# Scattering expert results to a row per pick, norms by chunks, and counts in bf16 at the tail of a four-layer transformer kernel

## The reference

```
x = _layernorm(x + _L0_attn_ref(x, ...))     # causal attention, 16 heads
x = _layernorm(x + _L0_ffn_ref(x, ...))      # 6 layers of window attention and feed-forward
x = _layernorm(x + _L1_attn_ref(x, ...))     # circular memory
x = _layernorm(x + _L1_ffn_ref(x, ...))      # routed experts
```

```
bound = _circ_conv(x, bind_key)
hologram = jnp.einsum('ts,bsd->btd', decay_matrix, bound)    # d ** (t - s) for s <= t
retrieved = _circ_corr(hologram, unbind_key)
```

```
probs = jax.nn.softmax(xf @ router_w.T, axis=-1)
topw, topi = jax.lax.top_k(probs, K)
topw = topw / (topw.sum(-1, keepdims=True) + 1e-06)
...                                          # sort by expert and weight, rank < capacity is kept
eo = jnp.einsum('ecf,efd->ecd', jax.nn.silu(g) * u, wd)
out = jnp.zeros_like(xf).at[st].add(gathered * (sw * keep)[:, None])
```

## Time and profile before

| | |
|---|---|
| three runs | median 2456.55 us (2451.24 to 2464.27) |
| profiled execution | 2461.72 us, span 2459.9 us |
| busy in the span | PE 2049.9 us (83%), DVE 1858.0 (76%), ACT 1636.6 (67%), POOL 1226.2 (50%) |
| first 2193 us | not touched by the change |
| 2193.6 to 2257.4 us | residual, norm b, memory, norm c |
| 2257.4 to 2323.5 us | routing |
| 2323.5 to 2403.2 us | the eight experts |
| 2403.2 to 2459.9 us | gathering the results, last norm, store |

### The profile page before, as it was taken

How to read it: one execution, slowest core, us unless ns; L and a number is a source line. 1 busy time by engine, 2 the same in 40 slices (tenths; PEclk the granted TensorE clock), 3 DMA queues, 4 the chain that set the end, 5 groups by cost and what they waited for, 6 DMA issues and landing times. The chain is left out here.

```text
span 2459.9 us, 55624 instructions
## 1 busy us (share of the span) xinstructions
PE 2049.9 (83%) x20371; PEld 1369.4 (56%) x20371; DVE 1858.0 (76%) x3667; ACT 1636.6 (67%) x3009; POOL 1226.2 (50%) x1091
## 2 busy tenths in 40 slices
PE   4389889638999999999999999999999999843390
PEld 2133333214677776777766767766767766632260
DVE  4555663249999999999999999999999999524523
ACT  2035655427888888888888888888888888712020
POOL 0100000047766777776777776677776677300115
PEclk8569997769999999999999999999999999966595
DMA  2403110031110112110211011111211011003102
GB/s 80 89 5 40 26 17 3 3 128 34 36 36 28 36 36 76 32 36 28 81 36 36 28 60 51 33 36 36 72 36 36 28 36 36 27 17 92 50 29 55
DMA packets 70913, 103.25 MB, mean 42 GB/s; under 512 B 21686, under 2 KB 45884, under 8 KB 70108
## 3 DMA queue, kind: packets, MB, share of 16 engines
q1 hardware_dynamic: 68980, 96.29, 14.4%
q0 software_dynamic: 1664, 3.41, 0.6%
HBM read 41.66 MB, written 8.06 MB: 20 GB/s over the span
## 5 line engine op out<-in xcount | busy, mean ns | idle before, releaser
L755 PE MATMUL pA<-layer_weights,x_feature_major 128*128 128x512 f32 x768 | 399.9, 603 | 32.3 <-DMA window_mask<-in_mask_dram 16.2
L1328 POOL TENSOR_TENSOR qk<-rot_cos,rot_sin 128x512 f32<-128x512 f32 x256 | 323.4, 1274 | 155.7 <-DVE rot_sin L1129 155.7
L399 ACT ACTIVATE probs_by_key<-pT 128x512 f32<-128x512 f32 (+3 forms) x384 | 177.6, 490 | 225.8 <-PE pT L352 192.3
L1127 DVE TENSOR_TENSOR rot_cos<-pA,layer_tab 128x512 f32<-128x512 f32 x384 | 262.9, 685 | 77.6 <-ACT sq L968 71.4
L1338 POOL TENSOR_TENSOR qk<-qk,rnorm 128x512 f32<-128x512 f32 x256 | 263.4, 1045 | 88.7 <-DVE rnorm L1162 88.7
L417 DVE TENSOR_REDUCE minus_max<-pS 128x1 f32<-128x1024 f32 (+7 forms) x256 | 184.6, 754 | 128.0 <-PE pS L326 127.8
L968 ACT ACTIVATE sq<-pA 128x512 f32<-128x512 f32 x384 | 228.7, 596 | 67.7 <-PE pA L755 58.1
L1139 DVE TENSOR_REDUCE sumsq<-sq 128x8 f32<-128x512 f32 x384 | 253.6, 671 | 15.3 <-ACT sq L968 15.2
L1129 DVE TENSOR_TENSOR rot_sin<-pA,layer_tab 128x512 f32<-128x512 f32 x384 | 260.9, 680 | 0.0
L1028 ACT ACTIVATE probsT<-pD 64x512 f32<-64x512 f32 x384 | 226.6, 590 | 44.5 <-PE pD L796 41.0
L1345 POOL TENSOR_TENSOR probs<-probs,row_inverse 128x1024 f32<-128x1024 f32 x96 | 182.6, 1903 | 101.7 <-DVE row_inverse L1198 101.7
(11 more groups left out here) (281 smaller groups left out, 4447.4 us busy)
## 6 DMA issues: line engine op xcount, KB each, us to landing
v_shifted<-v SPq DMA_DIRECT2D x96, 384.0 KB, 3.5
v_shifted<-v SPq DMA_DIRECT2D x95, 128.0 KB, 3.4
layer_weights<-in_Wqkv_dram SPq DMA_DIRECT2D x24, 384.0 KB
q_stack<-stacked SPq DMA_DIRECT2D x72, 64.0 KB
k_stack<-stacked SPq DMA_DIRECT2D x72, 64.0 KB
stacked<-part SPq DMA_DIRECT2D x24, 128.0 KB, 1.9
layer_weights<-in_Wo_dram SPq DMA_DIRECT2D x6, 512.0 KB
w_gate<-in_wg_dram SPq DMA_DIRECT2D x8, 256.0 KB, 6.4
```

What stands on the lines that cost most here:

```text
L755: pe.matmul(A[c % 2][:, :], cols(X0f, s), slot(s, QKV_AT + 512 * c, 512), start=True, stop=True).then_inc(q_ready[c], 1)
L1127: dve.tensor_tensor(t1[c % 2][:, :].rearrange("p (h g d) -> p h g d", g=2, d=32), a, tabl[s % 2][:, j].unsqueeze(1).broadcast_to([P, 8, 2, ...
L1328: pool.tensor_tensor(qk(s, c), t1[c % 2][:, :], t2[c % 2][:, :], ALU.add).then_inc(added[c], 1)
```

## The change

It has three parts.

- `add_aside`, norm b, `circular_memory` and norm c become one block, `residual_and_memory`, that works in four chunks of four tiles. The aside is loaded in four DMAs. Norms take the sum of squares from ScalarE activations per tile with the negative mean as bias and an accumulated output; norm b is applied by ScalarE, norm c by VectorE. The bind and the unbind matrix are multiplied into one matrix beforehand and scaled by the gate, so that the scan reads the turned tokens straight from PSUM, and the residual is a fused 2 X + retrieved.
- In `routed_experts` the counts and the two summing matrices are bf16.
- `tokens_in` now holds each token twice, once per pick, in rows 1 to 4096 (row 1 + 32 p + 2 t + k for partition p, tile t, pick k), and row 0 serves empty slots. The slot index names the pick's row. After each expert GpSimd scatters its slots' rows (20 indirect DMAs in all) into `expert_rows`, which has the same layout and was filled with zeros; GpSimd's list has them behind later experts' gathers. Experts come to share a slot tile in halves, so odd experts write their 64-row part first. At the end SP reads `expert_rows` back in four plain DMAs of 512 KB. The last norm works in four batches of four tiles, VectorE for sums and ScalarE for squares and for the normalisation.

```diff
         def sb(name, shape, dt=F32):
...
+            for n in range(CH):
+                sp.dma_start(T[:, chunk(n), :], w["aside"][:, chunk(n), :]).then_inc(aside_in[n], 16)
...
+            def retrieve(n):
+                pe.wait_ge(scanned, n + 1)
+                if n == 0:
+                    pe.wait_ge(product_kept, 1)
+                for j in range(CT):
+                    t = CT * n + j
+                    mm = pe.matmul(OUT[n][:, j * P:(j + 1) * P], holo[:, t * P:(t + 1) * P], memM[:, :], start=True, stop=True)
                 mm.then_inc(out_ready, 1)
+
+            turn(0)
+            pe.wait_ge(loaded, 32)
+            pe.transpose(bank[4][:, 0:P], bindM[:, :], ident[:, :])
+            pe.transpose(bank[4][:, P:2 * P], unbindM[:, :], ident[:, :]).then_inc(matrices_turned, 1)
+            turn(1)
+            pe.wait_ge(matrices_kept, 1)
+            pe.matmul(bank[5][:, 0:P], turnedM[:, 0, :], turnedM[:, 1, :], start=True, stop=True).then_inc(product_ready, 1)
+            turn(2)
+            retrieve(0)
+            turn(3)
+            for n in range(1, CH):
+                retrieve(n)
...
+            def square(k, n):
+                act.wait_ge(centred[k], n + 1)
+                for j in range(CT):
+                    t = CT * n + j
+                    act.activation(squares[:, t, :], Z[:, t, :], AF.Square, bias=negm[:, k, t:t + 1],
+                                   accum_out=sq[:, k, t:t + 1]).then_inc(squared[k], 1)
...
+            square(0, 0)
+            square(0, 1)
+            normalize(0)
+            square(0, 2)
+            normalize(1)
+            act.wait_ge(matrices_turned, 1)
+            act.activation(turnedM[:, :, :], bank[4][:, 0:2 * P].rearrange("p (k n) -> p k n", k=2), AF.Copy).then_inc(matrices_kept, 1)
+            square(0, 3)
+            normalize(2)
+            act.wait_ge(product_ready, 1)
+            act.wait_ge(gate_in, 32)
+            act.activation(memM[:, :], bank[5][:, 0:P], AF.Copy, scale=gate[:, 0:1]).then_inc(product_kept, 1)
+            normalize(3)
+            for n in range(CH):
+                square(1, n)
...
+            def residual(n):
+                dve.wait_ge(aside_in[n], 16)
+                dve.tensor_tensor(Z[:, chunk(n), :], T[:, chunk(n), :], X[:, chunk(n), :], ALU.add).then_inc(added[0], 1)
+                means(0, n)
...
+            def variance(k, n):
+                dve.wait_ge(squared[k], CT * (n + 1))
+                dve.tensor_scalar(ve[:, k, chunk(n)], sq[:, k, chunk(n)], 1.0 / D, EPS, ALU.mult, ALU.add).then_inc(eps_done[k], 1)
...
+            def scan(n):
+                dve.wait_ge(turned, n + 1)
+                first = n * CT * P
+                if n % 2:
+                    dve.wait_ge(scanned, n)
+                dve.tensor_tensor_scan(holo[:, first:first + CT * P], dcy[:, 5:6].broadcast_to([P, CT * P]), bank[n][:, :],
+                                       holo[:, first - 1:first] if n % 2 else 0.0, ALU.mult, ALU.add).then_inc(scanned, 1)
...
+            def remember(n):
...
+                dve.scalar_tensor_tensor(Z[:, chunk(n), :], X[:, chunk(n), :], 2.0, OUT[n][:, :].rearrange("p (t d) -> p t d", t=CT),
+                                         ALU.mult, ALU.add).then_inc(added[1], 1)
+                means(1, n)
...
+            residual(0)
+            residual(1)
+            variance(0, 0)
+            dve.wait_ge(gate_in, 32)
+            dve.tensor_scalar(dcy[:, 1:2], dcy[:, 0:1], -1.0, None, ALU.mult).then_inc(decay_set, 1)
+            dve.memset(dcy[:, 2:3], float(np.e)).then_inc(decay_set, 1)
+            residual(2)
+            variance(0, 1)
+            residual(3)
+            variance(0, 2)
+            dve.wait_ge(powered, 1)
+            dve.tensor_scalar(dcy[:, 4:5], dcy[:, 3:4], 1.0, None, ALU.add).then_inc(decay_step, 1)
+            dve.wait_ge(decay_step, 1)
+            dve.reciprocal(dcy[:, 5:6], dcy[:, 4:5]).then_inc(decay_step, 1)
+            dve.wait_ge(decay_step, 2)
+            scan(0)
+            variance(0, 3)
+            scan(1)
+            remember(0)
+            scan(2)
+            remember(1)
+            variance(1, 0)
+            scan(3)
+            remember(2)
+            variance(1, 1)
+            normalize(0)
+            remember(3)
+            variance(1, 2)
+            normalize(1)
+            variance(1, 3)
+            normalize(2)
+            normalize(3)
...
@@ -1610,18 +1715,28 @@
...
+            sp.dma_start(count_tab[:, :, :], w["before"]).then_inc(loaded, 16)
+            rows = w["tokens_in"][1:, :].rearrange("(p t k) d -> k p t d", p=P, k=TOPK)
+            for k in range(TOPK):
+                sp.dma_start(rows[k], X[:, :, :]).then_inc(x_stored, 16)
+            sp.dma_start(w["tokens_in"][0:1, :], X[0:1, 0, :]).then_inc(x_stored, 16)
...
+            for e in range(2):
+                load_expert(e)
+            results = w["expert_rows"][1:, :].rearrange("(p c) d -> p c d", p=P)
+            sp.wait_ge(zero_set, 1)
+            for k in range(TOPK):
+                sp.dma_start(results[:, k * TILES:(k + 1) * TILES, :], zero[:, :].rearrange("p (c d) -> p c d", d=D)).then_inc(zeroed, 16)
+            for e in range(2, EX):
+                load_expert(e)
+            sp.wait_ge(y_sent, 16 * SLOT_TILES)
+            for b, (t0, t1) in enumerate(LN_BATCHES):
+                sp.dma_start(got[:, t0:t1, :, :], results[:, TOPK * t0:TOPK * t1, :].rearrange("p (t k) d -> p t k d", k=TOPK))\
+                    .then_inc(arrived[b], 16)
...
-                pe.matmul(bank[6][:, 0:3], cst[:, SUM_AT:SUM_AT + P], cnt[:, :], start=True, stop=True).then_inc(counted, 1)
+                pe.matmul(bank[6][:, 0:3], count_tab[:, 1, :], cnt[:, :], start=True, stop=True).then_inc(counted, 1)
...
+                    pe.wait_ge(y_kept, 2 * (e - 1))
+                for col, row, k, first in CHUNKS[e % 2]:
                     for f in range(FC):
-                        mm = pe.matmul(Y[e % 2][0:k, c * P:(c + 1) * P], hT[e % 2][:, f, c * P:c * P + k], WD[:, e, f, :],
+                        mm = pe.matmul(Y[e % 2][row:row + k, col:col + D], hT[e % 2][:, f, first:first + k], WD[:, e, f, :],
...
+            def square(b):
+                act.wait_ge(centred, b + 1)
+                for t in range(*LN_BATCHES[b]):
+                    act.activation(squares[:, t, :], Z[:, t, :], AF.Square, bias=negm[:, t:t + 1], accum_out=sq[:, t:t + 1])\
+                        .then_inc(squared, 1)
...
+            square(0)
+            for b in range(1, len(LN_BATCHES)):
+                square(b)
+                normalize(b - 1)
+            normalize(len(LN_BATCHES) - 1)
...
+            pool.memset(zero[:, :], 0.0).then_inc(zero_set, 1)
...
+            def fetch(e):
...
+            def send(e):
+                pool.wait_ge(y_kept, 2 * (e + 1))
+                for t in range(5 * (e // 2) + 2 * (e % 2), 5 * (e // 2) + 2 + 3 * (e % 2)):
+                    pool.indirect_dma_start(out=w["expert_rows"], out_offset=bass.IndirectOffsetOnAxis(ap=idx[:, t:t + 1], axis=0),
+                                            in_=yo[:, t, :], in_offset=None).then_inc(y_sent, 16)
+            for e in range(4):
+                fetch(e)
+            pool.wait_ge(zeroed, 32)
+            for e in range(EX):
+                if e + 4 < EX:
+                    fetch(e + 4)
+                send(e)
...
+            for b, (t0, t1) in enumerate(LN_BATCHES):
                 pool.wait_ge(eps_done, b + 1)
                 pool.tensor_tensor(rstd[:, t0:t1], ve[:, t0:t1], half[:, t0:t1], ALU.pow).then_inc(rooted, 1)
-            due = {6: 0, 10: 1, 14: 2}
-            for t in range(TILES):
-                for k in range(TOPK):
-                    c = k * TILES + t
-                    pool.indirect_dma_start(out=got[:, t, k, :], out_offset=None, in_=w["expert_out"],
-                                            in_offset=bass.IndirectOffsetOnAxis(ap=gat[:, c:c + 1], axis=0)).then_inc(arrived[t], 16)
-                if t in due:
-                    root(due[t])
-            root(3)
-            root(4)
+                pool.wait_ge(rooted, b + 1)
+                pool.tensor_tensor(shift[:, t0:t1], negm[:, t0:t1], rstd[:, t0:t1], ALU.mult).then_inc(shifted, 1)
...
+            def summed(b):
+                t0, t1 = LN_BATCHES[b]
+                dve.wait_ge(arrived[b], 16)
+                pair = got[:, t0:t1, :, :]
+                dve.tensor_tensor(pair, pair, wt[:, :, t0:t1].rearrange("p k t -> p t k").unsqueeze(3).broadcast_to([P, t1 - t0, TOPK, D]), ALU.mult)\
+                    .then_inc(y_sum, 1)
+                dve.wait_ge(y_sum, 3 * b + 1)
+                dve.tensor_tensor(Z[:, t0:t1, :], pair[:, :, 0, :], X[:, t0:t1, :], ALU.add).then_inc(y_sum, 1)
+                dve.wait_ge(y_sum, 3 * b + 2)
+                dve.tensor_tensor(Z[:, t0:t1, :], Z[:, t0:t1, :], pair[:, :, 1, :], ALU.add).then_inc(y_sum, 1)
+                dve.wait_ge(y_sum, 3 * b + 3)
```

(20 more changed lines are left out.)

252 lines of the change are left out of this document (106 added, 146 removed).

## The result

| | before | after |
|---|---|---|
| median | 2460.41 us | 2389.23 us (2380.55 to 2408.77, 4 runs) |
| ratio | | 0.9721, 95% interval 0.9682 to 0.9761 |
| profiled execution | 2461.72 us, span 2459.9 | 2380.55 us, span 2378.7 |
| from the first load of the residual to the end | 266.3 us | 210.2 us |

The changed kernel is faster by 2.8%, 71 us in the medians. Two later comparisons of the same two kernels gave 0.9731 (0.9666 to 0.9796) and 0.9686 (0.9637 to 0.9735). The forecast was 54.8 us less, 2401.8 us, taken from a median of 2456.55 us of three executions; a fourth, of 2485.87 us, moved the median of the comparison to 2460.41.

The account below looks back on a forecast made before the run. The last 266 us were taken as bound by serial whole-tensor operations, float32 count waits and 32 final gathers. Savings 26.0 + 5.4 + 23.4 = 54.8 off 2456.55 gave 2401.8 us, range 2388 to 2420.

Parts of the forecast that it names:

- Its length stays 79.7: Sign for the expert loop: no engine waits for a gather there and the loop keeps its 79.7 us.
- Part A: Residual, norm, memory, norm: 63.8 us becomes 37.8 by following VectorE's new queue, saving 26.0 (22.4 to 29.4).
- decay: Residual and memory block: VectorE waits for the decay and gate columns before the third residual, 3.3 us lost.
- squares of the last chunk: Residual and memory block: VectorE, after scan 0, waits for ScalarE's squares 3, 2.3 us lost.
- first output: Residual and memory block: retrieval 0 needs the product matrix ScalarE scales behind normalisation 2; VectorE loses 2.5 us.
- VectorE's work: Residual and memory block: residuals, second sums, scans, variances, normalisations and decay column together take VectorE 25.2 us.
- Part B: Routing: a bf16 matmul replaces the float32 pair in 15 threshold steps, 0.34 us each; 5.4 saved with the offsets.
- Part C: Experts and end: scatters hidden beside experts; after the last expert's rows 33.4 us instead of 56.8, saving 23.4 (19 to 26).
- ScalarE as the pace: Rival, memory block and last norm: accumulating squares cost 0.9 us, not 0.46, adding 15 us, 2417; chance 0.12.
- Slow landing: Rival at the end: scatters land 2 us later, four reads take 4.8 each, 7 us more, 2409; chance 0.12.
- GpSimd as the bound: Rival in the expert loop: scatters of 5.2 us instead of 1.24 would eat the whole gain; slower than before, chance 0.02.
- The gain given back: Rival for the touched stretches: within 0.5% because each stretch's last engine, not the chains, was the bound; chance 0.02.

Follow-up runs that it names:

- both small edits: Changed kernel with gate and decay loaded ahead of the residual's first chunk, and routing's token transposes ahead of TensorE's wait for constants: 2393.67 us, ratio 0.969 to the kernel before.

## Why the prediction was right, step by step

**Where it comes from.** The three stretches gave 27.8 (forecast 26.0), 6.4 (5.4) and 25.1 us (23.4), less 2.8 for the logits and 0.4 in the expert loop: 56.1 against 54.8. In part that is luck: the three stretches gave 4.5 us more than their terms, and two losses that the sum doesn't have took 3.2 back. In the two later profiles, where the logits were fast, the stretch gave 57.0 and 57.8. In its own stages each part alone gave the same as in the whole, within 0.8 us. "Its length stays 79.7" was wrong for the expert loop by 0.4 to 1.6 us: a stall of 1.2 to 1.4 us ahead of the fourteenth silu, with a cause that is open.

**Part A, 36.0 for 37.8.** First chunk 3.17 (2.9), decay 3.62 (3.3), squares of the last chunk 1.95 (2.3), first output 3.05 (2.5), small waits 0.8 (1.1): 12.6 against 12.1. VectorE's work was the term mis-sized: 25.2 in the sum, and 36.0 - 12.6 - 0.5 = 22.9 in the trace, where 0.5 is the block's end. A normalisation of four tiles took 1.11 to 1.18 and not 1.27, the fused addition from PSUM 0.67 and not 0.75, and the small operations overlap their neighbours: 0.17 long, the next one 0.08 later. An accumulating square costs ScalarE 0.385 from one to the next where 0.46 was taken. Its groups by form in the changed kernel (total us, mean ns), and one square in the timeline:

```profile
L1484 ACT ACTIVATE squares_bc<-summed_bc,negative_mean 128x128 f32<-128x128 f32 x32 | 12.4, 389 | 14.3 <-DVE negative_mean L1535 14.3
L1872 ACT ACTIVATE tokens<-summed_c,shift_d,rstd_d 128x128 f32<-128x128 f32 x16 | 6.6, 481 | 1.5 <-POOL shift_d L1908 1.4
...
L1484 ACT ACTIVATION_READ_ACCUMULATOR squares_bc<-summed_bc,negative_mean 128x1 f32 x32 | 6.0, 187 | 0.0
```

```profile
2173.71 0.38 ACT L1484 ACTIVATE squares_bc<-summed_bc,negative_mean 128x128 f32<-128x128 f32 x1
2174.00 0.18 ACT L1484 ACTIVATION_READ_ACCUMULATOR squares_bc<-summed_bc,negative_mean 128x1 f32 x1
2174.09 0.39 ACT L1484 ACTIVATE squares_bc<-summed_bc,negative_mean 128x128 f32<-128x128 f32 x1
```

The read-out is an instruction of its own of 0.187 us, as the upper bound had it, but it begins before the square's shown end and the next square before the read-out's, so that only 0.09 us lie between the start of the one and of the other. The normalisation, 1.65 for four, was taken at 1.7.

What the prediction's walk did not tell is which wait mattered. It said that behind the wait for the decay stand two residuals and ScalarE's squares, which is so; but with the decay early the first chunk comes later and ScalarE's queue ends hardly sooner, so that removing the longest wait gained about 0.3 us against the mean, less than the spread of the block from one execution to the next.

**Part B, 6.4 for 5.4.** The bf16 matmul and its load end 0.19 us after the start where 0.25 was taken, and VectorE's wait fell by 0.40 per step and not 0.34. Over 15 steps that is the whole difference. The 3 MB more were hidden in B2, where no engine waited for them; with the scatter alone B1 was 0.7 to 0.8 us longer than before, of which 0.2 are the logits' and the rest has no experiment.

**Part C, 31.6 for 33.4.** The first data 9.0 us after the last rows (9.5): GpSimd woke in 0.28 and not 0.8, a scatter lands 2.25 after its start and not 2.8, the first 512 KB took 3.97 and not 3.3. VectorE's four batches took 14.3 (14.8), the tail behind them to the last normalisation 5.5 (5.2), the store 2.7 (3.9), which is the largest single miss of this part. Scatters cost what gathers do, 0.97 and 0.30 against 0.94 and 0.30.

**The rivals.** ScalarE as the pace: a square at 0.385 is far from the 0.9 it needed. Slow landing: the four reads arrived ahead of VectorE, which after the first never waited for one. GpSimd as the bound: a scatter takes 1.27 us and not 5.2; GpSimd is busy for 36 of the expert loop's 80.1 us. The gain given back, or slower than before: the ratio is 0.9721.

**The rule of the Trainium skill** ("ScalarE: Activation LUTs", Rules for kernel authors: additions and multiplications on VectorE) was set aside for the last norm because VectorE paces that stretch. By the measurement E is 0.3 to 0.6 us shorter by the rule, so the rule was on the better side. The prediction counted VectorE's 3.8 us and not what the queue order costs: with the normalisations on ScalarE the last squares stand behind them, and VectorE waited 2.31 us for those.

**What is left over.** The medians of the three comparisons fell by 71.2, 69.6 and 73.6 us, the touched stretch by 56 to 58. Of the time saved, 71.2 us, the sum of the prediction has 54.8; 1.3 of the 16.4 us between lie in the stretch that it adds up, and 15.1 outside of it. The 71.2 us lie outside the 45.8 to 62.2 that the bounds of its parts allow, and the measured 2389.2 us only 1 us above the lower end of the stated range, 2388 to 2420. The range reaches so far down for the spread of the three executions, not for anything that the change does outside its stretch, so that the time fell inside the range is luck; that the stretch fell by what was forecast is not. The step that put all before 2193.61 us at nothing because its code is untouched had no measurement behind it. Of the two profiled executions, attention up to norm a, of the kernel before:

```profile
68.00:481.80 413.80, 333.61 (x2169) 134.62 (x2169) 211.07 (x329) 186.41 (x405) 12.21 (x14) 0.80 0.16 25
175.00:200.00 25.00, 24.34 (x133) 9.33 (x132) 11.18 (x16) 11.67 (x25) 0.40 (x1) 0.64 0.32 41
```

and of the changed kernel:

```profile
68.00:456.30 388.30, 304.63 (x2169) 126.06 (x2169) 210.55 (x328) 185.34 (x405) 12.23 (x14) 0.88 0.19 27
175.00:200.00 25.00, 22.47 (x176) 9.28 (x173) 16.43 (x25) 15.34 (x33) 0.40 (x1) 1.00 0.38 49
```

It is the same 2169 matmuls at a mean granted clock of 0.80 or 0.88, with whole stretches at 0.64 in the one and 1.00 in the other. In the kernel before, its repetition and the three with one part alone attention took 394 to 419 us, mean 405.9; in the nine kernels with the whole change 388 to 408, mean 395.5. In all fourteen its length follows its granted clock: 0.78 with 419.2 us, 0.80 with 413.8, 0.84 with 404.7, 0.86 with 395.1, 0.88 with 387.7 to 389.2. What sets the clock is not shown. The ranges overlap from 394 to 408, and the changed kernel alone spreads over 16 us, so chance is at work, and the profiles weren't all taken on the same chip. Against chance alone speak a difference of 10 us between the means, and the five comparisons with the whole change (the three above, both small edits, and the last norm on VectorE): each fell by 13 to 16 us more than its stages account for, three of them against the same executions of the kernel before. With one part alone the medians fell by 24.7, 10.5 and 29.8 us where the stages have 27.0, 7.0 and 25.8, 2.3 less to 4.0 more. No experiment here touched it, and it stays open.

## What to carry to other kernels

Cut a row of whole-tensor operations into chunks and write out each engine's queue: the sum of the walk was right to 1.8 us in 37.8, mostly with prices from rows of the same or a doubled shape. But a walk gives the length and not the worth of a wait: the longest wait, taken away, came back at two other places, and only a kernel without it showed that. When such an edit moves the mark from which a stage is read, read it from the first issue, and hold it against several executions of the old order. Where a GpSimd DMA must be issued per tile anyway, issue it on the side where it lies beside other work: 17 scatters under the experts' matmuls cost at most the 0.4 to 1.6 us by which the loop grew, the same 17 behind them cost 22 us.

## What the runs showed of the hardware

- ScalarE's accumulated sum costs one instruction more. It is shown 0.187 us long, but starts 0.29 us after its square, and the next square 0.09 after it: 0.385 us from square to square, 0.09 of them for the read-out.
- GpSimd's power on 128 x 4 took 1.01 us, and 1.86 (2363.50) while VectorE multiplied and added with two inputs from SBUF; the small product behind it 0.52 for 0.20. The Trainium skill has such a case in "SBUF — State Buffer", Who interferes with whom: a VectorE instruction with two SBUF inputs contends with a GpSimd one that reads SBUF. The trace agrees: with the last norm on VectorE, whose batch normalisation has one input from SBUF, the power beside it took 1.03. In the changed kernel the last batch's power took 1.01, but the slow ones weren't free: ScalarE waited 1.05 and 0.39 us for GpSimd's products, and the last batch's squares stand behind these in its queue. With 1.01 and 0.20 they would by these rows have begun when their means were ready, at 2370.4 and not at 2371.13, an estimate of 0.7 us that no run checks.
- With the loads of the gate and decay columns (0.5 KB each) ahead of the residual's, VectorE had the first 256 KB chunk 4.12 and 4.18 us after its own issue in two executions, and 3.13 to 3.28 in the eight others.
- The 32 pairs of the logits took 6.5 us or 3.4 in the same code, and attention 388 to 419 us, both by the granted clock (0.50 and 0.85; 0.88 to 0.78).
- With every condition in the code met, ScalarE stood still for 8.4 and 7.9 us ahead of the same silu in two executions of one kernel, and for 1.3 to 1.45 us ahead of another in all seven executions with the whole change and early scatters, though never with a part alone. The cause wasn't found.
